# A hybrid transformer block on one core: VectorE's decay multiplies, scans and addition to x in another order

## The reference

```python
zxbcdt = u @ in_proj_w.T
z, xBC, dt = ...                       # 256, 512 and 32 columns
xBC = silu(conv4(xBC) + conv_b)        # causal, 4 taps
x, B, C = ...                          # 32 heads x 8, 128, 128
y = ssd_chunked(x * dt, A * dt, B, C, 32)
y = layernorm(y) * ln_w * silu(z)
return y @ out_proj_w.T
```

## Time and profile before

| | us |
|---|---|
| median of 3 runs | 2785.82 (2782.82 to 2787.51) |
| the profiled execution | 2776.01 |
| its span, first to last instruction | 2774.2 |
| TensorE busy | 2428.7 (88%) |
| VectorE busy | 1959.3 (71%) |
| ScalarE busy | 1469.9 (53%) |
| GpSimd busy | 1296.4 (47%) |
| mean granted TensorE clock | 0.905 of full speed |

### The profile page before, as it was taken

How to read it: one execution, slowest core, us unless ns; L and a number is a source line. 1 busy time by engine, 2 the same in 40 slices (tenths; PEclk the granted TensorE clock), 3 DMA queues, 4 the chain that set the end, 5 groups by cost and what they waited for, 6 DMA issues and landing times.

```text
span 2774.2 us, 62048 instructions
## 1 busy us (share of the span) xinstructions
PE 2428.7 (88%) x21968; PEld 1784.7 (64%) x21968; DVE 1959.3 (71%) x5809; ACT 1469.9 (53%) x2778; POOL 1296.4 (47%) x1816
## 2 busy tenths in 40 slices
PE   4999999999999969979974999999999977988991
PEld 3666555665556548868863666666667656886881
DVE  3887888878888748856656566676666657885666
ACT  1555555555555546645552556565555646654550
POOL 0444455445544437766652324242333305774661
PEclk9999999999999986769996899999989987768996
DMA  7443444334443301113332000000000000112336
GB/s 161 63 59 49 59 59 59 56 51 59 59 59 53 42 29 47 47 56 89 91 100 83 2 2 2 2 2 2 2 2 2 2 2 29 48 51 78 91 89 192
DMA packets 118421, 140.68 MB, mean 51 GB/s; under 512 B 21452, under 2 KB 79953, under 8 KB 118000
## 3 DMA queue, kind: packets, MB, share of 16 engines
q1 hardware_dynamic: 101232, 102.68, 19.9%
q0 software_dynamic: 16896, 34.12, 3.6%
HBM read 45.85 MB, written 40.54 MB: 31 GB/s over the span
## 4 chain that ended last, share of the span: by engine, by line
PE 52%; DVE 19%; issue 10%; POOL 9%; ACT 7%; DMA 2%; SPq 1%; DVEq 0%; POOLq 0%; ACTq 0%
DVE state L1846 4%; POOL probs_t L562 3%; PE psum L1655 3%; POOL acc L568 3%; PE psum L476 3%; PE psum L1219 3%; DVE x_sb L1393 3%; PE psum L543 2%; PE psum L582 2%; PE psum L1193 2%; PE psum L1194 2%; PE psum L1703 2%; PE psum L1195 2%; PE psum L653 2%; DVE psum L485 2%
## 5 line engine op out<-in xcount | busy, mean ns | idle before, releaser
L485 DVE CUSTOM_DVE_ANT_0 psum<-psum,causal 128x512 f32<-128x512 f32 (+3 forms) x1024 | 481.7, 512 | 148.6 <-PE psum L476 145.5
L553 ACT ACTIVATE probs_t<-psum 128x512 f32<-128x512 f32 (+1 forms) x768 | 388.8, 523 | 356.8 <-PE psum L543 355.8
L562 POOL TENSOR_SCALAR_AFFINE_SELECT probs_t<-probs_t 128x256 f32<-128x256 f32 x512 | 189.8, 407 | 455.8 <-ACT probs_t L553 455.8
L1328 POOL DMA_INDIRECT y_tok<-yb,xb x272 | 265.8, 977 | 161.8 <-issue 128.0
L476 PE MATMUL psum<-ls,qs 96*128 96x512 f32 (+3 forms) x1024 | 323.8, 359 | 10.0 <-DVE mx_raw L485 6.3
L543 PE MATMUL psum<-qs,ls 98*128 98x512 f32 (+3 forms) x1024 | 311.9, 348 | 4.4 <-ACT probs_t L553 2.4
L476 PEld LDWEIGHTS psum<-ls,qs 96*128 96x128 f32 x1024 | 182.5, 194 | 185.3 <-DVE mx_raw L485 88.4
L996 POOL DMA_INDIRECT x_slot<-pay,pos_i x256 | 254.2, 993 | 93.3 <-issue 74.3
L2071 POOL TENSOR_SCALAR dt_r<-dt_v 128x128 f32<-128x128 f32 x16 | 9.2, 576 | 438.5 <-DVE dt_v L1767 438.5
L543 PEld LDWEIGHTS psum<-qs,ls 98*128 98x128 f32 x1024 | 177.7, 192 | 42.4 <-ACT probs_t L553 29.1
L1292 DVE TENSOR_TENSOR bh<-psum,bs 128x512 f32<-128x512 f32 x136 | 94.1, 692 | 139.2 <-ACT bs L1254 135.2
(11 more groups left out here) (336 smaller groups left out, 6805.5 us busy)
## 6 DMA issues: line engine op xcount, KB each, us to landing
qs<-q_h SPq DMA_DIRECT2D x96, 256.0 KB, 5.4
xb<-x_slot SPq DMA_DIRECT2D x272, 66.0 KB
y<-y_tok SPq DMA_DIRECT2D x32, 512.0 KB, 3.5
qs<-q_l SPq DMA_DIRECT2D x48, 256.0 KB, 5.6
qs<-r_h SPq DMA_DIRECT2D x32, 256.0 KB, 6.2
y_tok<-yb,xb POOLq DMA_INDIRECT x272
x_sb<-in_x SPq DMA_DIRECT2D x16, 256.0 KB, 5.4
qs<-r_l SPq DMA_DIRECT2D x16, 256.0 KB, 5.7
```

The costliest lines, as they stand in the source:

```text
L485: last = dve.tensor_tensor_reduce(out=bank[n % 3][:, at:at + w_q], in0=bank[n % 3][:, at:at + w_q], in1=causal[:, L - w_q:L], scale=1.0, s ...
L553: act.activation(probs_t[:, i % 2, h % HG, UNIT_AT[k]:UNIT_AT[k] + UNIT_COLS[k]], bank[3 + m % 2][:, 0:UNIT_COLS[k]], ACT.Exp).then_inc(s[ ...
L562: last = pool.affine_select(out=p[:, :, at:at + P], in_=p[:, :, at:at + P], compare_op=ALU.is_ge, fill=0.0, base=0, pattern=[[0, 2], [1, P ...
L1328: pool.indirect_dma_start(out=y_tok[f][:, :], out_offset=bass.IndirectOffsetOnAxis(ap=xb[:, j2, k, D:D + 1].bitcast(I32), axis=0), in_=yb[ ...
```

## The change

On VectorE, in the state-space stage's `batch`, the calls `mix(b, 6)` and `mix(b, 7)`, which stood between the scans, now stand ahead of all of them. `out_add(b - 1)` moves from behind the last scans to between the second and the third call of `scan`. `shift_vector(b + 2)` moves from behind the fourth call of `scan` to ahead of it. Nothing else is changed.

```diff
                 mix(b, 5)
+                mix(b, 6)
+                mix(b, 7)
                 scan(b, 0)
                 scan(b, 1)
-                mix(b, 6)
+                if has_before(b):
+                    out_add(b - 1)
                 scan(b, 2)
-                mix(b, 7)
-                scan(b, 3)
                 if left > 1:
                     shift_vector(dve, b + 2)
-                if has_before(b):
-                    out_add(b - 1)
+                scan(b, 3)
                 y_join(b)
```

## The result

The changed kernel takes 2809.9 us (median of 4 executions, 2808.4 to 2811.9) against 2784.3 us before (median of 4, 2772.4 to 2787.5): 1.0097 times, 95% interval 1.0069 to 1.0125. Measured once more later: 1.0112 (1.0069 to 1.0155). It is slower, by 26 us, 1%.

The account below looks back on a forecast made before the run. TensorE was taken to bound each batch, with the shift-to-silu(z) chain nearly as late. Chain and edge batches +11.9 us plus clock +30.5 gave +42.4 on the 2785.8 us median: 2828 us, range 2797 to 2848.

Parts of the forecast that it names:

- The prediction's +11.9 us: State-space stage without the clock: thirteen batches with later `from_state` +11.3, batches 0 and 14 −2.4, batch 15 +3.0.
- the chain shift, norm, silu of z: Ahead of `from_state`: VectorE's shift 1.96 us later delays ScalarE's silu(z), so `from_state` starts 0.77 to 0.95 us later.
- The clock: At `from_state`: the new 2.0 us TensorE idles bring 7 drops of the granted clock at 4.36 us each, +30.5 us.
- rival C: At `from_state`: nearly every new idle, 10 to 13, pulls the clock down; +56 to +69 us, 2841 to 2855; 12%.
- A: At `from_state`: about half the new idles, 4 to 9, pull the clock down; +29 to +51 us, 2815 to 2837; 50%.
- B: At `from_state`: new idle mostly too short or well placed, 0 to 3 clock drops; +12 to +25 us, 2798 to 2811; 26%.
- D: At L1640: changed batch length removes up to eight old clock drops of 4.36 us, so faster, 2763 us; 6%.
- E: At `from_state`: the silu(z) chain is not last, the delay vanishes, time within 5.6 us of before; 6%.

Follow-up runs that it names:

- the threaded order: Kernel before with VectorE ordered scan 0, multiply 6, scan 1, shift, multiply 7, scan 2, addition, scan 3: 2781.1 us against 2786.1; repeated 2947.1 against 2945.4.
- the last test: Changed kernel with the matmul that clears the first chunk's output in `from_state` done four times instead of once: 3005.9 us against 2945.4, ratio 1.0223.

## Why the prediction was right, and where its sum was not

**What bounds, and the chain: right.** The prediction's +11.9 us rests on `from_state` waiting for the chain shift, norm, silu of z. The shift came 1.97 us later (1.96 predicted), the new idle is 1.97 to 2.00 us (2.0 predicted), thirteen times, released by L2017. That this chain costs, and not the scans, is shown by the run with the shift ahead of the addition; that it had slack before, by the run with the shift alone. With the cost of the falls taken off (0.43 us for each us), the thirteen batches take 12.1 us more in all (11.3 predicted), 0.93 each. Batch 14 gains 0.9 us (at most 1.2 predicted). Batch 0 lies ahead of this stretch; there too `from_state` waits 3.2 us for the silu of z, where the prediction had it beneath TensorE's end, and it starts at 1558.23 of the span in place of 1558.47, 0.2 us sooner and not 1.2. Batch 15 waits for its scans:

```profile
2308.24 0.60 PE L1706 MATMUL psum<-x_dec,zero 128*32 128x256 f32 x1 [5.77 <-DVE state L1846]
```

Its `from_state` starts 10.85 us after the end of exponential 7, in place of 7.80, +3.05 (+3.0 predicted); that exponential comes 0.5 us sooner in the batch, so the batch takes 46.96 us against 44.39, +2.6, with a fall of 20.5 us in both. L1682 waited 0.27 us, not 0.16 (1.02 − 0.86).

**The clock: the size of the term near by luck, its working wrong.** The prediction took 7 new falls behind L1706, by the share 8 of 15, at 4.36 us each, +30.5, and left the old ones alone. Measured were three other things. (1) 12 of the 13 new idles are followed by a fall, the upper end (rival C's count). (2) Each costs next to nothing, where 4.36 was taken over from L1640 with bounds of 0 and 5.5; the step that failed is "`from_state` and the sums and turns of the next batch, is all TensorE's own time": `from_state` is bound by its reads, and the fall ends with it. (3) The falls at L1640 rose from 8 to 14, 92.2 us at the lower clock to 136.5; at 0.43 us per us that is 44.3 x 0.43 = +19.0 us. The sum of the trace: 12.1 (chain) − 0.9 (batch 14) + 2.6 (batch 15) + 19.0 = 32.8, which is what the stage grew by (750.0 − 717.2). The medians lie only 25.6 us apart, since the profiled execution of before was one of its shorter ones. So the clock's term, put at 30.5, was 19.0 in the trace, and by the medians 25.6 − 13.8 = 11.8. That a term which the prediction had not priced stood in for the one that it had is why the time still fell into the range, 26 us slower in place of the 42 of the forecast.

**Rivals.** A, the forecast, gave 2815 to 2837; the measured 2809.9 lies below it, in the band of B (2798 to 2811), though B's reason (the new idle brings few falls) is false. C's count is right, its price not. D and E are out. None of them asks whether the falls at L1640 become more.

**What stays open.** Why the falls at L1640 rose. The new idle at L1706 isn't needed for it: the threaded order has none and 14 falls, the multiplies alone have an idle of 2.9 us at another place and 6. Nor is a fall at L1706 needed: ahead of batch 3 of the changed kernel `from_state` has none, and there is one of 10.2 us at the batch's L1640. Whether that idle adds to the falls in the changed kernel is not shown; without it, in the run with the shift ahead of the addition, there were 10 and 11. Over all orders with an idle of 2.08 us at L1640 there were from 6 to 14 falls in 15, and in the threaded order 14 and 11 in two profiles of the same program, so the length of the idle doesn't decide. Nor does the length of a full-clock batch by itself: of about 47.7 us there were 6 falls with the multiplies alone and 14 in the last test. The Trainium skill, "TensorE: Matmul & The Clock Gate", section "What's actually happening", calls the monitor free-running; that fits, but no run here shows by what rule the idles meet it.

## What to carry to other kernels

When work is reordered on an engine that is not the bound, ask which small instruction stands behind the moved work and who waits for it: here a 0.14 us shift, delayed by 2 us, cost more than the waits that were removed, and moving its call ahead turned +1.0% into −0.6 to −0.9%. Price a change of the clock by the work that it will cover: a stretch that is bound by its reads doesn't feel it. And judge such an order by batches at full clock as well as by the time: the threaded order, with 44.3 us among the shortest of these, had the least certain total, its executions lay up to 70 us apart.

## What the runs showed of the hardware that I had not expected

- Matmuls that read fp32 elements of the state spread out, in steps of 512 and 16 elements, took 3.9 us for 27 records at 1.2 and at 2.4 GHz alike; with adjacent elements 1.69 us at 2.4 GHz and 3.14 us at 1.2 GHz.
- Idles of about 2 and of 2.9 us in every batch over 286 us, with the granted clock at 1.00 throughout; in another order, idles of 0.66 and 1.14 us a few us apart, with the clock at 0.51 over the next 10 us.
- Where TensorE is dense, a us at the lower clock cost 0.42 to 0.44 us: batches with falls of 3.4, 6.8, 10.2 and 17.1 us took 1.4, 3.0, 4.4 and 7.3 us more between L1640 and `from_state` than those at full clock (the first three in the run with the shift ahead of the addition, the last in the kernel before).
- Equal programs were some 160 us longer in one comparison, in stages that no edit touched, with this stage at 704 against 700 us.
